# A routed feed-forward layer: return gathers that add in flight, outputs stored by pairs of slots, weights asked for two experts ahead

## The reference

```python
x = x + xattn(layernorm(x), ctx)                 # 8-bit quantise, dequantise, product
h = layernorm(x)
scores = sigmoid(h @ gate_w.T)                   # 64 scores; 4 of 8 groups, then 8 experts a token
cw[token, expert] = 2.5 * score / sum(of the 8)  # 0 for the other 56
y = sum over experts of cw * ((silu(h @ Wg.T) * (h @ Wu.T)) @ Wd.T)     # Wg, Wu 176 x 256
out = x + y + shared(h)
```

## Time and profile before

| | |
|---|---|
| median of 3 runs | 372.45 us (370.97 to 374.95) |
| profiled execution | 372.08 us, span 370.1 us |
| busy: PE, DVE, ACT, POOL | 267.1, 267.0, 168.5, 165.6 us |
| instructions on PE, DVE, ACT, POOL | 1431, 640, 407, 164 |
| moved by DMA | 86.23 MB, mean 233 GB/s |

### The profile page before, as it was taken

The page is one execution under the profiler, slowest core; times in us unless marked ns, Lnnn a source line. Parts: engine busy times, 40 slices in busy tenths (PEclk is TensorE's granted clock), DMA queues, the critical chain, the costliest instruction groups (busy, mean ns, idle before and its releaser), DMA issues.

```text
span 370.1 us, 7966 instructions
## 1 busy us (share of the span) xinstructions
PE 267.1 (72%) x1431; PEld 217.3 (59%) x1432; DVE 267.0 (72%) x640; ACT 168.5 (46%) x407; POOL 165.6 (45%) x164
## 2 busy tenths in 40 slices
PE   0101479979959499999999996898999989990000
PEld 0001165444748388888888885687888878880000
DVE  4799779996436268888887885565788887888832
ACT  1071542310126156667766764455676666660000
POOL 5015410427777778770000000445302773788882
PEclk9999999998979889999999999798999999997555
DMA  7999960004967479799757796898948899774134
GB/s 236 409 425 428 425 265 3 0 0 141 339 236 252 159 257 333 252 299 283 228 177 245 213 273 192 263 280 257 298 128 269 265 309 294 217 224 136 57 118 137
DMA packets 49241, 86.23 MB, mean 233 GB/s; under 512 B 5676, under 2 KB 38220, under 8 KB 47180
## 3 DMA queue, kind: packets, MB, share of 16 engines
q1 hardware_dynamic: 18652, 41.10, 32.0%
q10 hardware_dynamic: 24432, 26.12, 22.3%
q0 software_dynamic: 6144, 18.88, 15.3%
HBM read 46.07 MB, written 40.01 MB: 233 GB/s over the span
## 4 chain that ended last, share of the span: by engine, by line
PE 35%; DMA 13%; issue 12%; POOL 11%; DVE 10%; SPq 4%; POOLq 1%; ACT 1%; ACTq 1%; DVEq 1%
PE bank L1095 14%; PE bank L1134 13%; POOL xs L477 7%; PE bank L1120 4%; PE bank L1089 3%; DMA d_ring<-w_down 3%; DMA rows<-xs 3%; DMA early_c<-w_gu 3%; POOL xw L493 2%; POOL s_int L493 2%; SPq L361 1%; DMA xs<-xw,sidx 1%; SPq L364 1%; DVE gtop L778 1%; DMA ys<-y 1%
## 5 line engine op out<-in xcount | busy, mean ns | idle before, releaser
L1134 PE MATMUL bank<-d_ring,early_c 88*128 x336 | 93.8, 404 | 6.4 <-ACT early_c L594 5.3
L308 DVE TENSOR_TENSOR gu_lo<-early_c,gu_hi 128x704 fp32r<-128x704 f32 x87 | 76.9, 884 | 1.0 <-ACT gu_hi L304 0.6
L477 POOL DMA_INDIRECT xs<-xw,sidx x64 | 66.1, 1033 | 24.1 <-issue 23.2
L493 POOL DMA_INDIRECT early<-ys,yidx x24 | 26.2, 1094 | 102.4 <-DMA ys<-y 96.0
L1134 PEld LDWEIGHTS bank<-d_ring,early_c 88*128 88x128 f32 x336 | 60.5, 198 | 19.0 <-issue 12.6
L304 ACT ACTIVATE gu_hi<-early_c 128x704 fp32r x87 | 68.0, 782 | 5.9 <-issue 5.8
L930 DVE TENSOR_SCALAR y<-bank,rows 128x256 f32<-128x256 f32 x84 | 40.6, 483 | 34.2 <-PE bank L1134 32.7
L1095 PE MATMUL bank<-gu_hi,r_hi 128*128 128x352 f32 x170 | 63.8, 375 | 0.7 <-DVE r_lo L314 0.7
L1095 PE MATMUL bank<-gu_hi,r_lo 128*128 128x352 f32 x170 | 56.2, 331 | 0.0
L1095 PE MATMUL bank<-gu_lo,r_hi 128*128 128x352 f32 x170 | 56.1, 330 | 0.0
L594 ACT ACTIVATE early_c<-bank 88x256 f32<-88x256 f32 x84 | 31.9, 380 | 49.9 <-PE bank L1120 34.0
(11 more groups left out here) (199 smaller groups left out, 291.3 us busy)
## 6 DMA issues: line engine op xcount, KB each, us to landing
ys<-late SPq DMA_DIRECT2D x16, 1024.0 KB, 23.4
rows<-xs ACTq DMA_DIRECT2D x89, 160.0 KB, 3.3
early_c<-w_gu SPq DMA_DIRECT2D x37, 352.0 KB, 3.9
ys<-y ACTq DMA_DIRECT2D x22, 512.0 KB, 4.2
d_ring<-w_down SPq DMA_DIRECT2D x36, 176.0 KB
xc<-x SPq DMA_DIRECT2D x2, 512.0 KB, 4.0
xc<-ctx_kn SPq DMA_DIRECT2D x1, 1024.0 KB, 9.3
xs<-xw,sidx POOLq DMA_INDIRECT x64
```

What stands on the lines that cost most here:

```text
L308: v.tensor_tensor(gu_lo[:, b:b + 1, :], gu_ring[:, bass.ds(nth % R, 1), :], gu_hi[:, b:b + 1, :].bitcast(fp32), ALU.subtract).then_inc(glo ...
L477: pool.indirect_dma_start(out=xs, out_offset=bass.IndirectOffsetOnAxis(ap=sidx[:, c, at:at + 1], axis=0), in_=xw[:, c, :], in_offset=None, ...
L493: pool.indirect_dma_start(out=back[k][:, c, :], out_offset=None, in_=ys, in_offset=bass.IndirectOffsetOnAxis(ap=yidx[:, c, at:at + 1], axi ...
L1134: ins = pe.matmul(OB[b][:, 0:H], iT[:, b, s, :], d_ring[:, place, s, :], start=(s == 0), stop=(s == 1))
```

## The change

1. **The return.** All gathers go into `fin`, with an addition on the way (`compute_op=ALU.add`). `back_in` is now a semaphore for each chunk, and a gather waits until the gather of the rank before has landed in the same chunk. VectorE's additions at the end are gone; SP stores a quarter of `out` when its two chunks have eight gathers each.
2. **Stores.** `y` holds four pairs of slots. ScalarE stores a pair (256 KB) in the slots r = 0 and r = 2 of a quad, each behind the landing of the store before. The ranks' waits are counted in pairs.
3. **SP's ring.** SP asks for gate and up weights of expert n+2 while it serves expert n (`LEAD = 2`), and reads the registers of four experts with three loads. A second table, `gu_first_tab`, says from which slot on a place is free, and holds back loads for experts that do not exist. VectorE makes it with seven small operations ahead of the loop.

```diff
-        y = sb("y", [P, 2, R, H])
...
+        y = sb("y", [P, 4, 2, H])
+        zero = sb("zero", [P, C * H])
...
-        back_in = [sem(f"back_in{k}") for k in range(TOPK - 1)]
-        final_in = [sem(f"final_in{a}") for a in range(LAST)]
+        back_in = [sem(f"back_in{c}") for c in range(C)]
...
+            LEAD = 2
...
-            e, first = used_expert(R), first_slot(1)
             rings = sp.value_load(sizes[0:1, 1:2], min_val=0, max_val=E // R - 1)
-            quads = quads_of(sp)
-            sp.wait_ge(glo_ok, first)
-            load_gu(sp, e, 0)
+            sp.load(used, used_tab[0:1, R:2 * R + LEAD])
+            sp.load(gu_firsts, gu_first_tab[0:1, 1:1 + R + LEAD])
+            for n in range(LEAD):
+                sp.wait_ge(glo_ok, after_slot(gu_firsts[n]))
+                load_gu(sp, number(sp, used[n]), n)
+            announce(gu_in, 0, 2, gu_there)
             with sp.Fori(0, E // R - 1) as i:
                 with sp.If(i < rings):
-                    e, first = used_expert(i * R + R), first_slot(i * R + 1)
+                    sp.load(used, used_tab[0:1, bass.ds(i * R + R, R + LEAD)])
+                    sp.load(firsts, first_tab[0:1, bass.ds(i * R + 1, R)])
+                    sp.load(gu_firsts, gu_first_tab[0:1, bass.ds(i * R + 1, R + LEAD)])
                     for r in range(R):
-                        e_next, first_next = used_expert(i * R + (R + r + 1)), first_slot(i * R + (r + 2))
-                        sp.wait_ge(glo_ok, first_next)
-                        load_gu(sp, e_next, (r + 1) % R)
-                        announce(gu_in, r, i + 2, gu_there)
-                        sp.wait_ge(out_ps, first)
-                        load_down(sp, e, r)
+                        sp.wait_ge(glo_ok, after_slot(gu_firsts[r + LEAD]))
+                        load_gu(sp, number(sp, used[r + LEAD]), (r + LEAD) % R)
+                        announce(gu_in, (r + 1) % R, i + (3 if r == R - 1 else 2), gu_there)
+                        sp.wait_ge(out_ps, after_slot(firsts[r]))
+                        load_down(sp, number(sp, used[r]), r)
                         announce(d_in, (r - 1) % R, i + (1 if r == 0 else 2), down_there)
-                        e, first = e_next, first_next
...
             for a in range(LAST):
-                sp.wait_ge(y_sum, a + 1)
+                for c in range(a * CL, (a + 1) * CL):
+                    sp.wait_ge(back_in[c], TOPK * 16)
                 sp.dma_start(chunks(out)[:, a * CL:(a + 1) * CL, :], fin[:, a * CL:(a + 1) * CL, :]).then_inc(done, 16)
...
+            pool.wait_ge(sh_fin, C)
             for k in range(TOPK):
...
                 for c in range(C):
-                    arrived = back_in[k] if k < TOPK - 1 else final_in[c // CL]
+                    if k:
+                        pool.wait_ge(back_in[c], k * 16)
                     pool.indirect_dma_start(
-                        out=back[k][:, c, :], out_offset=None, in_=ys,
+                        out=fin[:, c, :], out_offset=None, in_=ys,
                         in_offset=bass.IndirectOffsetOnAxis(ap=yidx[:, c, at:at + 1], axis=0),
-                        bounds_check=(QUADS + 1) * QROWS - 1, oob_is_err=True).then_inc(arrived, 16)
+                        bounds_check=(PAIRS + 1) * PROWS - 1, oob_is_err=True, compute_op=ALU.add).then_inc(back_in[c], 16)
...
-                    if r == 0:
-                        act.wait_ge(y_st, i * 16 + 32)
-                        act.wait_ge(y_ok, i * R + 1)
-                        store_quad(i, slice(1 - odd, 2 - odd))
+                    if r % 2 == 0:
+                        last = (odd * 2 + r // 2 - 1) % 4
+                        act.wait_ge(y_st, i * 32 + (32 + 16 * (r // 2)))
+                        act.wait_ge(y_ok, i * R + (r + 1))
+                        store_pair(i * 2 + (r // 2), slice(last, last + 1))
...
+            step(v.tensor_scalar(padding[:, :], padding[:, :], 3.0, None, ALU.add))
+            settle()
+            step(v.tensor_scalar(beyond_last[:, :], first_ps, slots[:, 0:1], padding[:, 0:1], ALU.is_ge, ALU.mult))
+            settle()
+            step(v.tensor_tensor(gu_first_tab[:, :], beyond_last[:, :], first_ps, ALU.add))
...
-            v.wait_ge(sh_fin, C)
-            for k in range(TOPK - 1):
-                v.wait_ge(back_in[k], C * 16)
-                step(v.tensor_tensor(fin[:, :, :], fin[:, :, :], back[k], ALU.add))
-                settle()
-            for a in range(LAST):
-                cs = slice(a * CL, (a + 1) * CL)
-                v.wait_ge(final_in[a], CL * 16)
-                v.tensor_tensor(fin[:, cs, :], fin[:, cs, :], back[TOPK - 1][:, cs, :], ALU.add).then_inc(y_sum, 1)
```

More of the change, by code:

```diff
@@ L168, in xattn_moe_kernel @@
         quad_tab = sb("quad_tab", [1, QUADS + 1, 4, R], i32)
-        used_tab = sb("used_tab", [1, E + 1], i32)
-        first_tab = sb("first_tab", [1, E + 1], i32)
+        used_tab = sb("used_tab", [1, USED], i32)
+        first_tab = sb("first_tab", [1, USED], i32)
+        gu_first_tab = sb("gu_first_tab", [1, USED], i32)
+        slots = sb("slots", [1, 1])
+        padding = sb("padding", [1, 1])
+        beyond_last = sb("beyond_last", [1, USED])
         sizes = sb("sizes", [1, 2], i32)
@@ L358, in _, with after_slot @@
             sp.wait_ge(regs_ok, 1)
[L360 to L364, removed]
+            LEAD = 2
+            used = [sp.alloc_register(f"sp_used{n}") for n in range(R + LEAD)]
+            firsts = four_registers(sp, "sp_first")
+            gu_firsts = [sp.alloc_register(f"sp_gu_first{n}") for n in range(R + LEAD)]
+            quad_used = four_registers(sp, "sp_quad_used")
+            def after_slot(register):
+                return sp.snap(register, min_val=0, max_val=2 * P - 1) & (2 * P - 1)
             def announce(loaded, place, loads, there):
@@ L368, in announce @@
                 sp.sem_inc(there, 1)
-            experts = [used_expert(r) for r in range(3)]
+            sp.load(quad_used, used_tab[0:1, 0:R])
             for r in range(3):
-                load_gu(sp, experts[r], r)
+                load_gu(sp, number(sp, quad_used[r]), r)
+            load_down(sp, number(sp, quad_used[0]), 0)
             announce(gu_in, 0, 1, gu_there)
-            experts.append(used_expert(3))
-            load_down(sp, experts[0], 0)
+            load_gu(sp, number(sp, quad_used[3]), 3)
@@ L847, in _ @@
             step(v.tensor_copy(cum_col[:, :], bank[1][0:E, CUM:CUM + 2]))
+            step(v.tensor_copy(slots[:, :], bank[1][0:1, TOTAL:TOTAL + 1]))
             step(v.tensor_scalar(quads_f[:, 0:1], bank[1][0:1, TOTAL:TOTAL + 1], 1.0 / R, (R - 1.0) / R - 0.375, ALU.mult, ALU.add))
@@ L872, in _ @@
             step(v.tensor_scalar(nth_tab[:, :], nth_ps, last_used[:, 0:1], None, ALU.min))
-            step(v.tensor_scalar(sizes[:, :], quads_f[:, :], ROUND, ROUND, ALU.add, ALU.subtract))
+            step(v.tensor_scalar(quads_f[:, :], quads_f[:, :], ROUND, ROUND, ALU.add, ALU.subtract))
+            settle()
+            step(v.tensor_copy(sizes[:, :], quads_f[:, :]))
+            step(v.scalar_tensor_tensor(padding[:, :], quads_f[:, 0:1], float(R), slots[:, :], ALU.mult, ALU.subtract))
+            settle()
+            step(v.tensor_scalar(padding[:, :], padding[:, :], 3.0, None, ALU.add))
+            settle()
+            step(v.tensor_scalar(beyond_last[:, :], first_ps, slots[:, 0:1], padding[:, 0:1], ALU.is_ge, ALU.mult))
+            settle()
+            step(v.tensor_tensor(gu_first_tab[:, :], beyond_last[:, :], first_ps, ALU.add))
             v.wait_ge(need_ps, 1)
@@ L894, in _ @@
             v.wait_ge(max_ps, 1)
[L895 removed]
+            step(v.tensor_scalar(rank_quads[:, :], bank[0][0:1, TOP_ROW:TOP_ROW + TOPK], 1.0 / PROWS, -(PROWS + 1) / (2.0 * PROWS), ALU.mult, ALU.add))
             vector_out(v, 3)
@@ L927, in quad @@
                     v.wait_ge(out_ps, i * R + (r + 1))
-                    if r == 0:
-                        v.wait_ge(y_st, i * 16 + 32)
-                    v.tensor_scalar(y[:, odd, r, :], OB[r % 2][:, 0:H], rows[:, place, bass.ds(expert + H, 1)], None,
+                    if r % 2 == 0:
+                        v.wait_ge(y_st, i * 32 + (16 + 16 * (r // 2)))
+                    v.tensor_scalar(y[:, odd * 2 + r // 2, r % 2, :], OB[r % 2][:, 0:H], rows[:, place, bass.ds(expert + H, 1)], None,
                                     ALU.mult).then_inc(y_ok, 1)
```

55 lines of the change are left out of this document (26 added, 29 removed).

## The result

The changed kernel takes **386.36 us** (median of 4 runs, 385.73 to 389.07); the kernel before took 372.87 on the same chip. The ratio is **1.037 [1.030, 1.045]**. The forecast was 361, with 351 to 374 for the range: wrong in sign. The profiled execution took 386.81, its span is 385.1, 15.0 longer than before.

A forecast was written before the change was run, and what follows sets the result against it. GpSimd's queue of gathers was taken to set the end. 370.1 - 14.5 + 0.5 + 1.0 - 3.5 + 5.2 = 358.8, with 2.0 outside the span 360.8, 361.2 by the median, stated as 361; range 351 to 374.

The forecast's parts named there:

- I take the plain price, the row of the nearest form: GpSimd's cost of an adding gather: taken as a plain one's 1.01 us, between bounds of 1.01 and 2.02.
- dearer descriptors: Rival: an adding gather costs GpSimd half again as much, chain from rank 4 without slack, time 374, no change; chance 0.18.
- slower: Rival: every adding gather takes GpSimd 2.02 us, 47 steps of 2.32 from rank 2, time 398; chance 0.14.
- the signs of being wrong: A gather over 1.3 us on GpSimd, gathers waiting for their predecessors, or ScalarE waiting for a store to land.
- waits of gathers for their predecessors, put at nothing: On GpSimd, each gather's wait for the previous rank's on its chunk, 10.5 us behind against a 3.01 landing: costs nothing.
- Contention of adding gathers, +1.0 (0 to 5): Second half of the loop: adding gathers' extra transfers cause new waits for rows and weights, +1.0 us, between 0 and 5.
- The tail, -14.5: After the loop: 12.75 us from rank 7's earlier start, 1.05 from the stretched gather, 0.7 from the addition.
- The landing of the last gather, +0.5: End of the kernel: the last adding gather lands 0.5 us later, between 0 and 3.0.
- The stretching goes away with VectorE's additions: Tail gathers of 2.02 us return to 1.01 without VectorE's additions; the rival that they stay, 367 to 369, had 0.08.
- Twice the stores, +5.2: ScalarE in the loop: 21 more stores, 15 at full pace costing 0.35 us each, +5.2 us, between 0 and 7.4.
- Weights two ahead, -3.5: SP's queue from slot 39 on, slots 42 to 54: asking earlier and fewer register loads gain 3.5 us, between 0 and 6.8.
- At nothing: tables: Before the loop: seven tiny VectorE operations cost nothing, since first slots wait for scatters; without that cover about 1 us.

The follow-up runs named there:

- The return alone: Kernel before with only the return changed, gathers adding into the residual tile, stores and SP's queue as before: 386.20 us, ratio 1.036.
- ranks 2 and 3 adding: Kernel before with stores by pairs and gathers of ranks 2 and 3 adding into `fin`, the other six ranks added by VectorE: 370.15 us, ratio 0.994.
- ranks 0 to 2 adding: Kernel before with stores by pairs and gathers of ranks 0, 1 and 2 adding into `fin`, five ranks added by VectorE: 369.69 us, ratio 0.988.
- The pairs alone: Kernel before with only the stores changed to pairs of slots, plain gathers and VectorE's additions kept: 367.99 us, ratio 0.989.
- SP's part alone: Kernel before with only SP's queue changed, gate and up weights two experts ahead and registers read in batches: 375.59 us, ratio 1.009.
- Batching: Kernel before with SP's ten register loads for four experts drawn together into two, still one expert ahead: 371.57 us, ratio 0.996.
- both other edits and the pairs: Kernel before with stores by pairs, SP's weight announcements one step later and its register loads drawn together, one expert ahead: 367.16 us, ratio 0.980.

## Why the prediction was wrong, step by step

- **The failed step: "I take the plain price, the row of the nearest form".** Between 1.01 and 2.02 it chose the lower end; the runs show 1.56. The rival *dearer descriptors* had 1.5. Beside it stood the rule of the Trainium skill, "Collectives: The Full Stack", section "The bandwidth ceiling: the fold count and why AG ≠ RS ≠ AR", that the reduce step of a collective emits two read descriptors where a copy emits one. In time the trace agrees (three for two would be 1.5, an estimate from that page; measured are 1.56), in packets it does not, for those tripled. "Same rows, sizes and indices" was true and no argument: with all of them unchanged GpSimd's time rose by half. With 1.56, a step of 1.86, *slower*'s own sum gives 279.6 + 47 x 1.86 + 7.5 + 2.0 = 376.5, so the price makes some 15 of the 25 us by which the forecast missed. The other 10 are the next two points. Of the signs of being wrong two came, a gather over 1.3 us and ScalarE before a store; waits of gathers for their predecessors, put at nothing, did not: a gather that one released stood idle 0.30 us, like any other.
- **The rivals' times.** At a price of 1.5 the chains of both come out alike: 374 from rank 4, and from rank 2 279.6 + 47 x 1.80 + 7.5 + 2.0 = 373.7. *Slower* had the right chain, from rank 2 without a pause, and the wrong price, 2.02, which gave 398. With the measured step of 2.01 its sum is 383.6, 2.8 short of 386.36; rank 2 came 3.6 later than it took. That 386 lies between the two rivals is in part chance, since neither had gathers that add stretched by the loop. The chain's probability was too small (0.14).
- **Contention of adding gathers, +1.0 (0 to 5).** Too low. The return alone lengthened slots 8 to 83 by 7.6 us, the addition inside the change by 5.4 (204.9 against 199.5). The estimate of 0.4 us of all engines a gather was right (0.45 more); "nearly all the slack" was used up too: a DMA share of 0.96 from rank 2 on. What the forecast didn't have is that GpSimd's own step grows in the loop, 2.01 instead of 1.86: gathers up to 2.23 stand there, none above 1.56 after it.
- **The tail, -14.5.** With plain gathers and no additions its shape was right: GpSimd at 1.01, released by the last store. But rank 7 started at 348.33, not 339.9: slot 83 came 6.0 later, and its store landed 8.4 behind it, not 5.7. The forecast added the loop's terms to the end, +2.7 in sum; 6.0 was measured. The landing of the last gather, +0.5, was about +1.0: in the change 7.5 us pass from its start to the end of the span, before 7.2 with an addition of 0.69 among them.
- **The stretching goes away with VectorE's additions.** Right, and now shown by runs: after the loop each run has as many stretched gathers (1.5 to 3.0 us) as VectorE makes additions of 128 x 2048: seven; five with ranks 2 and 3 adding; four with ranks 0 to 2 adding; none without additions, where plain ones take 1.01 or 1.02 and adding ones 1.56. The page "SBUF — State Buffer" of the Trainium skill, section "Who interferes with whom", says that such additions did not stall DMA issue. The trace differs: 2.02 beside them stands against 1.01 without.
- **Twice the stores, +5.2.** The pairs alone lengthened slots 8 to 83 by 3.0 us, inside the bounds of 0 to 7.4 and no more than such a stretch varies by. That half a quad lands sooner was wrong (4.0 us for 256 KB); that it is in time held with the pairs alone and not beside adding gathers.
- **Weights two ahead, -3.5.** Wrong in sign: SP's part alone is 0.9% slower. Batching gained 3.7 us in slots 42 to 54, asking two ahead then cost 4.3 there, with a new wait of TensorE for down weights that the forecast didn't look for. "The transfers don't allow it" was too careful: both other edits and the pairs brought these slots to 34.3, the 34 that the forecast had as full engines.
- **At nothing: tables.** Nothing contradicts it: slot 4 starts at 129.54, before at 129.67.

## What to carry to other kernels

Before a DMA takes over an addition, ask who writes its list and whether that engine is the one that ends the program: here a gather dearer by 0.55 us on a queue without pauses cost more than all the additions that it replaced. When two bounds of an unknown price are far apart, work out the price at which the verdict turns and give the chances by that point; where a rule puts the price beyond it, the row of the nearest form is no reason to stay below. A gain in one stretch of a loop is read at the loop's last slot, not in the stretch: 5.2 us in slots 42 to 54 came out as 0.6 at slot 83.

## What the runs showed of the hardware

- An indexed gather of 128 rows of 1024 bytes took GpSimd 1.01 us plain and 1.56 us adding; adding rows of 512 bytes took 1.56 too. 64 of them had 3072 packets plain and 9216 adding, and filled all 16 DMA engines for 29.0 and 57.5 us, with the same bytes.
- Beside adding gathers the DMA engines were 0.96 busy in the loop at 232 GB/s; beside plain ones 0.82 at 259 (before) and 0.84 at 255 (the change without its addition).
- After the loop each addition of 128 x 2048 on VectorE went with one stretched gather on GpSimd, most of 2.02 us where 1.01 is undisturbed.
- A store of 256 KB landed in 4.0 us, one of 512 KB in 4.2.
- Three register loads of 6, 4 and 6 numbers took SP 3.6 us in one lump.
